# Moving the transform of the convolution spectrum from the set-up to the start of the second layer

## What is computed

```
x                       [4, 512, 256] f32;  ctx [4, 1601, 192] f32
layer 0:  x += attention(layernorm(x), ctx; 16 heads of 16)
          x += experts(layernorm(x); 8 experts, the best 2 of each token, inner 512)
layer 1:  x += block(layernorm(x), ctx):
              scores -> best 32 of 1601 -> softmax -> mean over 4 heads -> context c_t
              u = film_in(c_t, layernorm(x));  y = irfft(rfft(u, n=1024) * Kf, n=1024)[:512] + u * D_skip
              film_out, then a feed-forward 256 -> 1024 -> 256
          x += mixture attention(layernorm(x); 16 heads of 64, 8 value and output experts, the best 2)

Kf = rfft(K, n=1024),  K[d, l] = 2 Re sum_n dC[d, n] exp(dtA[d, n] * l),  l = 0..511
dtA = exp(log_dt) * A,   dC = C * (exp(dtA) - 1) / A        # depends on the weights alone
```

## Time and profile before

| | us |
|---|---|
| median of three runs | 2865.64 |
| the profiled execution, its own time | 2862.61 |
| its span, first to last instruction | 2860.8 |
| PE, DVE, ACT, POOL busy | 2277.7, 1464.1, 1456.8, 917.3 |
| mean granted clock of PE | 0.895 |

### The profile page before, as it was taken

The page is one execution under the profiler, slowest core; times in us unless marked ns, Lnnn a source line. Parts: engine busy times, 40 slices in busy tenths (PEclk is TensorE's granted clock), DMA queues, the critical chain, the costliest instruction groups (busy, mean ns, idle before and its releaser), DMA issues.

```text
span 2860.8 us, 36683 instructions
## 1 busy us (share of the span) xinstructions
PE 2277.7 (80%) x12668; PEld 1291.2 (45%) x12668; DVE 1464.1 (51%) x4388; ACT 1456.8 (51%) x2266; POOL 917.3 (32%) x473
## 2 busy tenths in 40 slices
PE   0567799999984899667899767899668898768997
PEld 0433222323222566336555446556446555446555
DVE  8756111121213111397575696574696564795563
ACT  2134477777771122384267582266582366681374
POOL 2023100101011111374058273076372085370094
PEclk9988899999996999858999868999768999769999
DMA  2044834443224111202113203013203023103022
GB/s 63 0 145 167 175 49 83 56 83 51 54 92 146 47 45 41 60 1 67 56 31 48 60 1 121 1 40 50 49 1 122 0 44 50 38 1 114 0 31 45
DMA packets 176516, 166.51 MB, mean 58 GB/s; under 512 B 84048, under 2 KB 147152, under 8 KB 176304
## 3 DMA queue, kind: packets, MB, share of 16 engines
q1 hardware_dynamic: 168816, 154.73, 23.2%
q0 software_dynamic: 7504, 9.35, 1.7%
HBM read 131.88 MB, written 32.32 MB: 57 GB/s over the span
## 4 chain that ended last, share of the span: by engine, by line
PE 45%; DVE 23%; POOL 11%; issue 8%; ACT 7%; DMA 4%; SPq 2%; DVEq 1%; POOLq 0%; another core or an unknown queue 0%; ACTq 0%
DVE sb_xnT L2358 5%; PE ps L1311 5%; POOL sb_arena L730 5%; PE ps L1322 5%; POOL sb_xtn L728 4%; ACT sb_arena L962 3%; PE ps L1493 2%; PE ps L1717 2%; PE ps L1665 2%; PE ps L1596 2%; PE ps L1506 2%; PE ps L1512 2%; PE ps L1735 2%; PE ps L1645 2%; PE ps L1654 2%
## 5 line engine op out<-in xcount | busy, mean ns | idle before, releaser
L962 ACT ACTIVATE sb_arena<-ps 128x1024 f32<-128x1024 f32 x416 | 402.7, 1021 | 121.2 <-PE ps L1311 115.1
L2358 DVE MAX8 sb_xnT<-sb_arena 128x8 f32<-128x60 f32 (+1 forms) x1728 | 246.8, 206 | 34.4 <-ACT sb_arena L1061 34.4
L2519 DVE TENSOR_REDUCE sb_arena<-ps 128x2 f32<-128x1024 f32 x128 | 156.2, 1223 | 203.3 <-PE ps L1735 203.0
L1311 PE MATMUL ps<-sb_arena 96*128 96x512 bf16 x832 | 234.8, 387 | 28.3 <-ACT sb_arena L962 14.3
L1564 PE MATMUL ps<-sb_arena,sb_xnT 32*128 32x400 f32 (+1 forms) x512 | 161.1, 715 | 111.6 <-ACT sb_arena L1061 107.7
L851 POOL TENSOR_TENSOR sb_arena<-sb_arena 128x1601 f32<-128x1601 f32 x56 | 176.5, 3152 | 161.6 <-DVE sb_arena L2346 158.1
L1322 PE MATMUL ps<-sb_arena 128*32 128x512 f32 x1664 | 225.1, 613 | 1.5 <-ACT sb_arena L962 1.5
L730 POOL TENSOR_TENSOR sb_arena<-sb_arena,sb_xtn 128x1024 f32<-128x1024 f32 (+1 forms) x112 | 208.4, 1861 | 8.8
L786 POOL DMA_INDIRECT taken_rows<-sb_taken,sb_slots x32 | 31.3, 977 | 547.9 <-DVEq L2116 539.3
L1146 ACT ACTIVATE sb_arena<-ps 128x512 f32<-128x512 f32 x256 | 151.9, 593 | 90.4 <-PE ps L1703 90.0
L728 POOL TENSOR_TENSOR sb_arena<-sb_arena 128x1024 f32<-128x1024 f32 (+1 forms) x16 | 24.1, 1506 | 533.6 <-DVEq L2476 528.3
(11 more groups left out here) (350 smaller groups left out, 4539.3 us busy)
## 6 DMA issues: line engine op xcount, KB each, us to landing
sb_arena<-k_spill SPq DMA_DIRECT2D x96, 208.0 KB, 8.1
sb_arena<-in_ctxT SPq DMA_DIRECT2D x12, 1601.0 KB, 7.3
sb_arena<-in_dft SPq DMA_DIRECT2D x5, 2048.0 KB, 7.6
k_spill<-sb_arena SPq DMA_DIRECT2D x12, 832.0 KB, 5.2
sb_arena<-in_w SPq DMA_DIRECT2D x16, 512.0 KB, 6.2
sb_arena<-in_idft SPq DMA_DIRECT2D x4, 2048.0 KB, 8.7
sb_arena<-in_wf SPq DMA_DIRECT2D x8, 1024.0 KB, 12.0
o_rows<-sb_arena SPq DMA_DIRECT2D x32, 256.0 KB, 2.3
```

The costliest lines, as they stand in the source:

```text
L962: A(probs0[:, 2 * (m % 4):2 * (m % 4) + 2, :], ps[:, 2 * (m % 2):2 * (m % 2) + 2, :], ACT.Exp).then_inc(pair_probs, 1)
L1311: ins = mm(ps[:, 2 * (m % 2) + i, :], k_stack[0:NSPLIT, h, k * P:(k + 1) * P], q_stack[0:NSPLIT, h, :], start=True, stop=True)
L2358: ins = V.max(cand[:, n % 2, 8 * j:8 * j + 8], s_sb[:, n % 6, c0:c0 + w])
```

## The change

The transform of `k_time` into the spectrum leaves the set-up and stands behind the experts. `k_time` is now written into `k_cos`, whose final contents come only later. In the set-up, DVE sorts part 1, then does `in_tokens(1)`, then sorts part 0. SP loads `ctxT` without a wait, and the weights after `setup_p` has reached 2. The 2 MB table is loaded again as `dft_k`, behind the last store of the experts, onto columns of the expert weights. PE does the 32 products after the four key groups of the first sequence in layer 1, into banks 0 to 3; ACT copies them out before its `deviation()` and the third key group; DVE makes `k_cos0` after its second layernorm. The semaphore `setup_done` is gone; `dft_k_loaded`, `spectrum_done` and `spectrum_ready` are new.

```diff
-        dft_s = at(o, [SEQ // P, 2 * SEQ]); o += SEQ // P * 2 * SEQ
-        s_e = at(o, [NPW])
-        k_time = at(o, [SEQ // P, DIM]); o += NPW
+        assert o <= CTX_AT
+        o = AFTER_CTX
+        s_e = at(o, [NPW]); o += NPW
         assert o <= ARENA
+        k_time = k_cos
+        dft_k = at(4096, [SEQ // P, 2 * SEQ])
 # SP
-            const(dft_s[:, :, :], a["dft"].rearrange("(c p) f -> p c f", p=P))
...
             sp.dma_start(xt[:, :, :], a["x"][0]...).then_inc(in_x, 16)
-            sp.wait_ge(setup_done, 1)
             sp.dma_start(ctxT[:, :, :], a["ctxT"][0]...).then_inc(in_ctx, 16)
+            sp.wait_ge(setup_p, 2)
             sp.dma_start(wq0[:, :, :], ...).then_inc(in_w, 16)
...
                 sp.dma_start(y_rows[i * P:(i + 1) * P, :], y_out[:, i % 2, :]).then_inc(y_stored[i % 2], 16)
+            sp.dma_start(dft_k[:, :, :], a["dft"].rearrange("(c p) f -> p c f", p=P)).then_inc(dft_k_loaded, 16)
             sp.wait_ge(batch_ended, 4)
             sp.dma_start(mask8, a["vmask"][0].partition_broadcast(P)).then_inc(mask_loaded, 16)
 # POOL, before its memsets
-            pool.wait_ge(setup_done, 1)
+            pool.wait_ge(setup_v, 9)
 # ACT, set-up
-            act.wait_ge(setup_done, 1)
 # ACT, keys_and_queries(b)
                 for n, (c0, w) in enumerate(COLS):
+                    if n == 2 and b == 0:
+                        act.wait_ge(spectrum_done, 1)
+                        half = FCH // 2
+                        spec_k = ps[:, 0:4, :].rearrange("p b (j d) -> p (b j) d", d=DIM)
+                        A(k_cos[:, :, :], spec_k[:, 0:half, :], ACT.Copy)
+                        A(k_sin[:, :, :], spec_k[:, half:FCH, :], ACT.Copy)
+                        act.drain().then_inc(spectrum_ready, 1)
                     if n == (1 if b else 2):
                         deviation()
 # PE, set-up
-            pe.wait_ge(setup_v, 9)
-            for j in range(FCH):
-                for c in range(SEQ // P):
-                    ins = mm(ps[:, 2 + j // 2, ...], dft_s[:, c, j * P:(j + 1) * P], k_time[:, c, :], ...)
-            ins.then_inc(setup_p, 1)
-            pe.wait_ge(setup_done, 1)
 # PE, input stage, between the queries and the keys
                 pe.wait_ge(in_ctx, 16 * b + 16)
+                pe.wait_ge(setup_v, 9)
 # PE, keys_and_queries(b), after the four context_item
+                if b == 0:
+                    pe.wait_ge(dft_k_loaded, 16)
+                    for j in range(FCH):
+                        for c in range(SEQ // P):
+                            ins = mm(ps[:, j // 2, ...], dft_k[:, c, j * P:(j + 1) * P], k_time[:, c, :], ...)
+                    ins.then_inc(spectrum_done, 1)
                 turn(b, xt, xn_ready, 0)
 # PE, at the head of each sequence of layer 1
                 pe.wait_ge(q1_ready, nth(b, q1_ready, 1))
+                pe.wait_ge(spectrum_ready, 1)
 # DVE, set-up
-                for n, part in enumerate((1, 0)):
-                    dve.wait_ge(setup_p, n + 1)
...
+                dve.wait_ge(setup_p, 1)
+                time_rows(1)          # the 16 copies of L1891
+                dve.sem_inc(in_xn, 1)
+                in_tokens(1)
+                dve.wait_ge(setup_p, 2)
+                time_rows(0)
                 done(9)
-                dve.wait_ge(setup_p, 3)
-                link(V.tensor_copy(k_cos[:, :, :], spec_k[:, 0:half, :]))
-                link(V.tensor_copy(k_sin[:, :, :], spec_k[:, half:FCH, :]))
-                ...                   # k_cos0, one row of k_sin
-                dve.drain().then_inc(setup_done, 1)
 # DVE, layer 1
                 layernorm(xn, xt, in_normal)
+                if b == 0:
+                    dve.wait_ge(spectrum_ready, 1)
+                    ...               # the same three small operations
```

More of the change, by code:

```diff
@@ L334, in program @@
         ramp = at(o, [LB + LA]); o += LB + LA
-        dft_s = at(o, [SEQ // P, 2 * SEQ]); o += SEQ // P * 2 * SEQ
-        s_e = at(o, [NPW])
-        k_time = at(o, [SEQ // P, DIM]); o += NPW
+        assert o <= CTX_AT
+        o = AFTER_CTX
+        s_e = at(o, [NPW]); o += NPW
         assert o <= ARENA
+        k_time = k_cos
+        dft_k = at(4096, [SEQ // P, 2 * SEQ])
+        assert 4096 + SEQ // P * 2 * SEQ <= S_AT
         k_spill = nc.dram_tensor("k_spill", [NBATCH, 3, DIM, KPAD], BF16).ap()
@@ L361, in program @@
         setup_p = early.enter_context(nc.semaphore("setup_p"))
-        setup_done = early.enter_context(nc.semaphore("setup_done"))
         def once(name):
@@ L388, in program @@
         late_loaded = once("late_loaded")
+        dft_k_loaded = once("dft_k_loaded")
+        spectrum_done = once("spectrum_done")
+        spectrum_ready = once("spectrum_ready")
         film_scaled = once("film_scaled")
@@ L1165, in _ @@
             mm, tr = nc.tensor.matmul, nc.tensor.transpose
+            pe.sem_inc(in_k_done, 1)
+            pe.sem_inc(in_xT_done, 1)
+            pe.sem_inc(in_norms_done, 1)
             for n, part in enumerate((1, 0)):
@@ L1542, in keys_and_queries @@
                     context_item(b, n)
+                if b == 0:
+                    pe.wait_ge(dft_k_loaded, 16)
+                    for j in range(FCH):
+                        for c in range(SEQ // P):
+                            ins = mm(ps[:, j // 2, (j % 2) * DIM:(j % 2 + 1) * DIM], dft_k[:, c, j * P:(j + 1) * P], k_time[:, c, :],
+                                     start=(c == 0), stop=(c == SEQ // P - 1))
+                    ins.then_inc(spectrum_done, 1)
                 turn(b, xt, xn_ready, 0)
@@ L1885, in setup_program, with time_rows @@
                 blocks = ps[:, :, :].rearrange("p k (g d a) -> p (k g) d a", d=4, a=LA)
-                for n, part in enumerate((1, 0)):
-                    dve.wait_ge(setup_p, n + 1)
+                def time_rows(part):
                     gs = slice(part * DIM // 8, (part + 1) * DIM // 8)
@@ L1892, in setup_program @@
                                                 blocks[LB * d:LB * (d + 1), gs, d, j::4])
-                link(ins)
-                done(9)
-                dve.wait_ge(setup_p, 3)
-                half = FCH // 2
-                spec_k = ps[:, 2:6, :].rearrange("p b (j d) -> p (b j) d", d=DIM)
-                link(V.tensor_copy(k_cos[:, :, :], spec_k[:, 0:half, :]))
-                link(V.tensor_copy(k_sin[:, :, :], spec_k[:, half:FCH, :]))
-                link(V.tensor_copy(k_cos0[:, :], k_cos[:, 0, :]))
-                link(V.tensor_copy(k_cos0[0:1, :], k_sin[0:1, 0, :]))
-                link(V.memset(k_sin[0:1, 0, :], 0.0))
-                dve.drain().then_inc(setup_done, 1)
-            setup_program()
+                    link(ins)
+                dve.wait_ge(setup_p, 1)
[4 more added lines that the diff above has]
+                time_rows(0)
+                done(9)
             IN_STEPS = 5
@@ L1923, in in_tokens @@
                     V.tensor_scalar(xn[:, t, :], xt[:, t, :], ln_mv[:, t, 0:1], ln_rstd[:, t:t + 1], ALU.subtract, ALU.mult).then_inc(in_xn, 1)
+            setup_program()
             def prepare(b):
@@ L1959, in _ @@
             V.memset(k_p[:, :, :, GKEYS:KPAD], 0.0)
-            dve.sem_inc(in_xn, 1)
             dve.sem_inc(in_k_parts, 1)
             dve.sem_inc(in_norms_read, 1)
-            in_tokens(1)
             with dve.Fori(0, NBATCH) as b:
@@ L2317, in _ @@
                 layernorm(xn, xt, in_normal)
+                if b == 0:
+                    dve.wait_ge(spectrum_ready, 1)
+                    link(V.tensor_copy(k_cos0[:, :], k_cos[:, 0, :]))
+                    link(V.tensor_copy(k_cos0[0:1, :], k_sin[0:1, 0, :]))
+                    link(V.memset(k_sin[0:1, 0, :], 0.0))
                 def settle(n):
```

5 lines of the change are left out of this document (removed).

## The result

The changed kernel takes 2833.82 us (median of 4 runs, 2824.87 to 2839.10), the kernel before 2866.10 (4 runs, 2865.42 to 2867.64). The ratio is 0.9887, 95% interval 0.9873 to 0.9901: 1.1% less. The forecast was 2834.5 in 2827 to 2846. The profiled execution took 2834.18 us, with a span of 2832.3, against 2862.61 before.

The account below looks back on a forecast made before the run. PE had 45% of the chain, no engine more; the change touched the set-up's end and layer 1's start. 2862.61 - 1.3 - 31.8 + 2.0 = 2831.5, plus 3.0 for the median: 2834.5 us, range 2829 to 2840, with rivals 2827 to 2846.

Parts of the forecast that it names:

- Part 1: Front of the set-up: without the 2 MB table behind it, the `phase` load lands sooner; 1.3 us saved, bounds 0 to 3.2.
- Part 2: Input stage brought forward: the queries end at 137.9 instead of 169.67, 31.8 us earlier, bounds 26.9 to 35.9.
- Part 3: Start of layer 1: the spectrum behind the experts, mostly in PE's hole, adds net 2.0 us, bounds -0.9 to +9.
- ACT's hold: Start of layer 1: ACT's two spectrum copies, drain and table load bring the square root 3.3 us late.
- The credit of 1.3 us for a warm PE: Start of layer 1: PE, after 14 us of work, turns x and forms queries at 2.4 GHz, winning 1.3 us.
- PE is idle for 3.7 us only, so I take 14.1: Start of layer 1: PE's wait before the 32 products is too short for its clock to fall; they take 14.1 us.
- the sum stays the same: Start of layer 1: sharing DMA engines with the table's load, the gathers add nothing, as the spectrum holds ACT longer.
- Rival (a): Start of layer 1: spectrum late, clock fallen, products 16 to 18 us; layer 1 7 to 9 us late, 2841; chance 0.18.
- (b): Input stage: the weights land late, at 135.8; 4 us less gain, 2838.5; chance 0.10.
- (c): Start of layer 1: spectrum wholly hidden, PE warm, nothing added; 2832, or 2829 with the fastest queries; chance 0.09.
- (d): Input stage: from its second sequence on, paced by something that has not moved, so the lead is lost; 2863; chance 0.03.
- (e): Whole kernel: PE's mean granted clock falls and eats the gain; 2871 at a fall of 0.025; chance 0.02.

Follow-up runs that it names:

- e6: The kernel before with the 2 MB table's load moved behind the set-up's other loads and the first x: 2861.36 us, ratio 0.9975.
- e2: The changed kernel with the first sequence's layernorm behind DVE's second copies instead of between the copies: 2850.20 us, ratio 0.9922.
- e3: The changed kernel with the input stage's weights loaded to columns of their own, without waiting for the time kernel's products: 2842.21 us, ratio 0.9898.
- e11: The changed kernel again, unedited, on another chip than its first repeat: 2832.62 us, ratio 0.9886 to the kernel before.
- e10: The changed kernel with table and weights loaded early, ACT's spectrum copies later, and 12 unread products keeping PE busy: 2825.21 us, ratio 0.9854.
- the first group: The follow-up runs e1 to e4, made on one chip together with the kernel before; ratios 0.9880 to 0.9922.
- e1: The changed kernel once more, nothing edited: 2840.89 us, ratio 0.9885 to the kernel before.
- e5: The changed kernel with ACT's two spectrum copies moved behind the square root and the copies of the turned x: 2832.91 us, ratio 0.9878.
- e12: The changed kernel with the spectrum's table loaded in pieces during the last experts, second comparison of that kernel: 2832.30 us, ratio 0.9882.
- e8: The changed kernel with the table loaded during the last experts and the weights loaded without waiting for the time kernel's products: 2827.89 us, ratio 0.9866.
- the early table: The changed kernel with the spectrum's table loaded in pieces during the last experts; alone 2827.30 and 2832.30 us in two groups, also combined with other edits.
- e4: The changed kernel without the spectrum (no table load, products or copies), so its result is not the convolution: 2837.86 us, ratio 0.9880.

## Why the prediction was right, step by step

**Part 1** (1.3 us earlier forecast): 2.27 measured, inside the bounds of 0 to 3.2, while the 1.3 was a choice between them. e6 alone gives 2.2, so the mechanism is shown.

**Part 2** (31.8): 33.66 - 2.27 = 31.4 measured. The path held at each step. DVE's layernorm cost nothing, and e2 shows what it would have cost; it took 3.9 us (118.48 to 122.35) and not the 6.3 taken from the kernel before, which left more room. The weights were the last release; the forecast time of 131.8 less the 2.27 of part 1 is 129.5, and PE started at 129.87. The queries took 6.14 us for 6.1; that it is so close is luck, since in the seven traces with this wait they took 5.3 to 6.3. e3 confirms the new wait, at 2.1 us. POOL's cover was tighter than I wrote, since its memsets ended 0.29 us before its square was released.

**Part 3** (2.0 us later): 2.1 measured at the first score, out of two terms of which neither is right. ACT's hold was forecast to bring the square root 3.3 us late; it was 2.3, with the table landed 8.3 us after its issue and PE done at 22.8 us behind the store (23.6 forecast). Of these 2.3 only 0.7 are ACT's: the late gathers brought DVE's variance 1.6 us later than before (25.4 us behind the store for 23.7), a term that the forecast had at nothing. The credit of 1.3 us for a warm PE failed: from square root to first score 8.20 us, 8.39 before. The step "PE has just worked for 14 us and may turn x and form the queries at 2.4 GHz" overlooked that ACT's 3.3 us of copies and table load are a hole for PE too; in it the clock falls. In the first trace it stays down through the first scores, so that at the MAX8 the loss was 3.9; in e11, where it came back sooner, 0.7. e10 shows that the credit is real once PE has no hole: 2.2 us from square root to first score. Two more statements of this part were wrong. "PE is idle for 3.7 us only, so I take 14.1": the idle time was 2.8, and even so the products took 17 us in three of six traces, those of the first group. It rested on a single fall, and that one was misread: a mean of 0.76 in the stretch from 1165 puts it at 1165.5, which is 5.0 us after PE's end and not 5.2; in e1 the clock fell inside 2.8. And "the sum stays the same" for the gathers: they started 1.8 us late, which in e5, where ACT is out of the way, leaves the square root 1.3 us late. That the table is the reason is not shown (e12).

**Rival (a)** was given 0.18, and it is what e1, e2 and e3 show, though with the table landed in time. Layer 1 then reaches its first score 5.3 us later than before, and the MAX8 7.5 us (priced at 7 to 9); by the medians no more than the forecast is lost. **(b)** did not happen (3.2 us for the last weights). **(c)** happened only with e8's edits. **(d)** is refuted: 33.7 us of lead at the queries are 37.1 at the end of the experts. In e1's trace the lead fell from 34.1 to 25.0 us by then, more than the 5 us that the prediction allowed, in the stages between, with no step of the change there. But the trace before is of another group; against the kernel before of their own groups the medians of e1 and e11 keep 29.6 and 34.0 us. **(e)** is refuted: the mean granted clock is 0.894 for 0.895, and in the groups of e1 and e11 the median clock of their runs is above that of the kernel before (0.895 for 0.892, 0.896 for 0.891). What is left of it is scatter. The four runs after have clocks of 0.893, 0.893, 0.894 and 0.898, and the last is the one of 2824.87 us. From the last store to the end of the span the two traces of the changed kernel needed 1705.3 us (e11) and 1714.8 (the first). The two of the kernel before, which e6 does not alter there, needed 1706.2 and 1714.3 (e6). So the fall of the lead from 33.2 to 28.5 us in layer 1 belongs to no step of the change.

The sum by traces: 2862.61 - 33.7 (queries) - 3.4 (up to the experts' end) + 3.9 (start of layer 1) + 4.7 (rest) = 2834.1. The first term is the change. Of the third 2.1 us, up to the first score, come again in e11 (2.2); the rest is the slow clock's length, which does not. The second and fourth are scatter, larger than the whole of part 3. That the total came out within a microsecond is partly luck; the 31 us are not.

Open: why the gather is late in four of the five traces with the early table, where e6 has its other 4 us, and what decides between 14 and 17 us of products behind the same hole. In all four traces of the first group, e4 with no products included, the clock fell 1.9 to 2.1 us after the key groups' end, and in no other trace sooner than 4.0 us after PE's last matmul ahead of the hole. So it goes with the group, by its chip or by something else that was different there.

## What to carry to other kernels

Work that has its whole inputs early and its first use late can be moved into a hole of its engine, but what pays is what the move lets start earlier; here that was the layernorm between two blocks of copies, a third of the gain. Count a hole in PE as waiting, then look at the granted clock behind it (here some 2 us, most of it queries at half speed), and look for the hole that your own work on another engine makes. A large load issued right behind a small one can hold up whoever waits for the small one: 2.2 us in the set-up. Before pricing a stretch by one trace, look at a second trace of the same kernel: at the MAX8 the cost of the spectrum was 0.7, 3.9 and 7.5 us in three.

## What was not expected of the hardware

- The granted clock fell 4.9 us after the end of the products in the changed kernel's trace (1140.3 to 1145.2, the latter by the mean of 0.77 over the 4 us shown), but 1.9 us after PE stopped in e1's (0.56 us busy in the stretch from 1135, and a mean of 0.91 over its 3 us: a fall at 1137.5). It then stayed at 0.50 for 13.7 us in the changed kernel's first trace and for 6.8 in e11's.
- A load of 2 MB issued 0.5 us behind one of 2 KB moved the landing of the small one from 3.7 to 5.9 us (e6 and before). A store of 128 KB landed after 1.7 us in some traces and after 3.6 in e12, with the same 200 KB load issued 0.36 us behind it; no run tells why.
- The table load of ACT sat directly in front of its ACTIVATE: 1.28 us, and the square root began 0.01 us behind it.
- DVE's normalising of four blocks took 1.38 us alone and 3.05 us beside POOL's memsets (e2).
